# A fused four-layer kernel: the setup of the weights and the first split of rows and context, made one block

## The chip, the cores and the metric

One core of a Trainium2 chip runs the whole program. The metric is the device time of one execution in microseconds (us), the median of several runs. The engines are PE (TensorE; its weight loads are PEld), DVE (VectorE), ACT (ScalarE), POOL (GpSimd) and SP (SyncE, which here only issues DMAs). SPq and ACTq are the instruction queues of SP and ACT, seen while they issue DMAs.

## The reference

Two cross-attention layers and two feed-forward layers on 32 sequences of 128 rows with 128 channels, with a context of 32 times 77 rows:

```
x = x + tanh(g_xattn[0]) * L0_xattn(layernorm(x), ctx, ctx)        # 16 heads of 8
x = x + tanh(g_ffn[0])   * L0_ffn(layernorm(x))                    # ternary weights, depthwise conv, silu
x = x + tanh(g_xattn[1]) * L1_xattn(ctx, layernorm(x), mask)       # 16 heads of 64
x = x + tanh(g_ffn[1])   * L1_ffn(layernorm(x))                    # 8 experts, top 2
weight_quant(w): scale = 1 / clip(mean(|w|), 1e-5); clip(round(w * scale), -1, 1) / scale
```

The precision of float32 is kept by splitting each operand of a product into a high half in float16 and a low half (the rest, in float16).

## The kernel before

The program is a row of blocks. At the end of a block all engines meet at a barrier. Inside a block each engine runs its own instructions in the order in which they are written, and semaphores order them against each other. The blocks that matter here are the first four:

1. `setup` loads everything. SP issues x in four parts, `w1`, `w2`, `w3` of the experts (`nat_moe`, `nat_w3`), then the context (`ctx`), and once all has landed it clears an 18 MB table in HBM (`tokens`). ACT issues 24 small and middle-sized loads (gates, feed-forward weights, the projections of both layers) before it computes anything. DVE takes the statistics of x and their inverse root (`rstd`), then sums the absolute feed-forward weights (`absum`); PE adds that sum over partitions (`bank[7]`), and DVE quantises the weights and makes the three conv taps (`tap_w`).
2. Still in `setup`, weights are turned. There is a list `tiles`; for tile k PE transposes into PSUM bank `k % NB`, ACT copies the high half out of the bank (`hi_done`), DVE takes the low half out of the bank (`lo_done`, for tiles that have one), and PE may use the bank again for tile k + NB when both have been counted. After the tiles come four products of `q1t` and `k1t` (`product_bank`) in the same ring of banks. NB is 6.
3. `split_transposed(... "split0")` normalises x and turns it, and turns the context. For a chunk k of 4 sequences DVE normalises (`normalise`), PE transposes into one of two banks, ACT copies twice (the whole in float32, the high half in float16), and POOL subtracts (`rows_xl`, the low half). The buffers are double: `normalise(k)` waits for PE's chunk k - 2, PE's chunk k waits for ACT's k - 2, ACT's for POOL's k - 2. Then the context goes the same way without DVE, while DVE takes the statistics of the context (`context_scale`).
4. `project0` makes queries, keys and values for the first attention; `attention0` follows.

In the tables of DVE below, L326 to L393 are `setup`, L440 is `normalise`, L1122 to L1128 are `context_scale`.

Of the kernel before, what the change touches and what calls it, by code (L numbers as in the profile page):

```python
# [5 lines left out]
FP16 = mybir.dt.float16  # L6
# [3 lines left out]
ALU = mybir.AluOpType  # L10
# [4 lines left out]
C = 77  # L15
H = 16
# [92 lines left out]
def setup(nc, a, w, bank):  # L109

    with Memory(nc, "setup", w.spent) as m:
# [31 lines left out]
        block = m.block()  # L143
# [32 lines left out]
        def tile_bank(k, src):  # L176
            p, t, n = src.shape
            return bank[k % NB][0:n, 0:t * p].rearrange("q (t p) -> q t p", p=p)

        def product_bank(g):  # L180
            return bank[(NT + g) % NB][:, :].rearrange("q (t p) -> q t p", p=128)

# [23 lines left out]
        def _(act):  # L206
# [21 lines left out]
            act.dma_start(nat_o0[:, 0], a["o0"]).then_inc(l1_in, 16)  # L228
            act.wait_ge(small_in, 12 * 16)
# [20 lines left out]
        def _(pe):  # L250

            pe.wait_ge(made, 2)
# [24 lines left out]
            for g in range(G):  # L277
                pe.wait_ge(hi_done, NT + g - NB + 1)
                pe.wait_ge(lo_done, lows(NT + g - NB + 1))
# [7 lines left out]
        def _(pool):  # L287
# [25 lines left out]

            pool.wait_ge(small_in, 12 * 16)
# [5 lines left out]
        def _(dve):  # L320
# [10 lines left out]
            rsqrt(dve, link, w.rstd[:], w.mv[:, :, 1], t1[:], t2[:])  # L331

# [73 lines left out]

def split_transposed(nc, w, bank, tag, jobs, before=None, after=None):


    with Memory(nc, tag, w.spent) as m:  # L410
        for at, job in enumerate(jobs):
            n, rows = job.name, job.rows
            job.normed = m.sb(f"normed_{n}", [rows, 2, CH, D]) if job.by else None
            job.whole = m.sb(f"whole_{n}", [128, 2, CH, rows])
            job.ready, job.turned, job.high, job.split = (m.sem(f"{x}_{n}") for x in ("ready", "turned", "high", "split"))
            job.banks = [bank[2 * at + u][:, 0:CH * rows].rearrange("p (c r) -> p c r", r=rows) for u in range(2)]
        chain = m.sem("chain")
        pre, post = (work(m) if work is not None else None for work in (before, after))
        block = m.block()

        def chunks(eng, job, body):


            if job.by == "vector":
                with eng.Fori(0, NCH // 4) as i:
                    for n in range(4):
                        body(i * 4 + n, n % 2)
            else:
                for k in range(NCH):
                    body(k, k % 2)  # L430

        def normalise(eng, job, k, u):
            eng.wait_ge(job.turned, k + 1)
            for c in range(CH):
                one = slice(k * CH + c, k * CH + c + 1) if isinstance(k, int) else bass.ds(k * CH + c, 1)
                if job.by == "gpsimd":
                    how = (job.rstd[:, one], job.shift[:, one], ALU.mult, ALU.add)
                else:
                    how = (job.mean[:, one, 0:1], job.rstd[:, one], ALU.subtract, ALU.mult)
                last = eng.tensor_scalar(job.normed[:, u, c:c + 1], job.src[:, one, :], *how)  # L440
            last.then_inc(job.ready, 1)

        @block.vector
        def _(dve):
            if pre is not None:
                pre(dve, linker(dve, chain))
            for job in jobs:
                if job.by == "vector":
                    chunks(dve, job, lambda k, u: normalise(dve, job, k, u))
            if post is not None:  # L450
                post(dve, linker(dve, chain))

        @block.tensor
        def _(pe):
            for job in jobs:
                def turn(k, u):
                    if job.by:
                        pe.wait_ge(job.ready, k + 1)
                    pe.wait_ge(job.high, k + 1)
                    for c in range(CH):  # L460
                        rows = job.normed[:, u, c] if job.by else job.src[:, k * CH + c]
                        last = pe.transpose(job.banks[u][:, c, :], rows, w.ident[0:job.rows, 0:job.rows])
                    last.then_inc(job.turned, 1)

                pe.sem_inc(job.turned, 2)
                chunks(pe, job, turn)

        @block.scalar
        def _(act):
            for job in jobs:  # L470
                def copy(k, u):
                    chunk = bass.ds(k * CH, CH)
                    act.wait_ge(job.turned, k + 3)
                    act.wait_ge(job.split, k + 1)
                    for dst in (job.whole[:, u], job.hi(chunk)):
                        if job.gain is None:
                            last = act.activation(dst, job.banks[u], ACT.Copy)
                        else:
                            last = act.activation(dst, job.banks[u], ACT.Identity, bias=job.bias, scale=job.gain)
                    last.then_inc(job.high, 1)  # L480

                act.sem_inc(job.high, 2)
                chunks(act, job, copy)

        @block.gpsimd
        def _(pool):
            for job in jobs:
                def low(k, u):
                    chunk = bass.ds(k * CH, CH)
                    pool.wait_ge(job.high, k + 3)  # L490
                    pool.tensor_tensor(job.lo(chunk), job.whole[:, u], job.hi(chunk), ALU.subtract).then_inc(job.split, 1)
                    if job.by == "gpsimd" and k + 2 < NCH:
                        normalise(pool, job, k + 2, u)

                pool.sem_inc(job.split, 2)
                if job.by == "gpsimd":
                    normalise(pool, job, 0, 0)
                    normalise(pool, job, 1, 1)
                chunks(pool, job, low)
# [95 lines left out]
def attention0(nc, w, bank, qst, kst, vals):  # L595
# [1559 lines left out]
```

## Time and profile before

| | us |
|---|---|
| median of 3 runs | 1308.46 (1308.11 to 1310.41) |
| the profiled execution: its time | 1310.83 |
| its span, first to last instruction | 1308.7 |
| `setup`, up to the last DVE instruction of the block | 0 to 59.1 |
| `split0` | 59.1 to 86.8 |
| `project0` | 86.8 to 135.3 |
| DVE busy in the 27.7 us of `split0` | 25.73 |
| PE, ACT, POOL busy in the same | 14.63, 14.49, 15.23 |

The profile is of one execution. A row of a timeline gives start, length, engine, source line, operation, what it writes and reads, how many instructions were merged, and in brackets how long the engine had been idle before it and what ended that.

### The profile page before, as it was taken

To read this page: it belongs to the slowest core of one execution; us is meant where nothing else is said; L and a number is where in the kernel's file an instruction comes from. 1 tells how busy PE (TensorE), PEld (TensorE's weight loads), DVE (VectorE), ACT (ScalarE), POOL (GpSimd) and SP (SyncE) were. 2 spreads that over 40 slices of the span, in tenths; PEclk is the share of its full clock that TensorE was granted. 3 is DMA by queue.
4 is the path that set the end of the run, shared out by engine and by line. 5 is a ranking of instruction groups with operands and counts; after the bars stand their busy time and mean duration, and the time that the engine had idled before them with its cause. 6 is when DMAs were issued, how large, how long until landed. Compare 5 with 4: busy or idle time off the path is not lost.

```text
span 1308.7 us, 36650 instructions
## 1 busy us (share of the span) xinstructions
PE 1035.4 (79%) x13473; PEld 815.3 (62%) x13473; DVE 878.0 (67%) x2479; ACT 876.3 (67%) x1830; POOL 879.7 (67%) x994
## 2 busy tenths in 40 slices
PE   0569899994887459999999999999999981288860
PEld 0445677772544248888887878788787860266640
DVE  5789788885886966666675667767666741266645
ACT  0559899982664548888887878878887861166540
POOL 1170799993676737768778788788878886357661
PEclk9859555556998579999999999999999985599995
DMA  9995000000222001111211322131212211222216
GB/s 219 255 284 123 8 16 15 17 17 5 38 44 49 1 1 30 31 34 27 50 33 39 47 37 57 32 62 34 51 39 39 55 34 50 79 67 78 81 35 193
DMA packets 188834, 78.67 MB, mean 60 GB/s; under 512 B 118463, under 2 KB 184938, under 8 KB 188667
## 3 DMA queue, kind: packets, MB, share of 16 engines
q1 hardware_dynamic: 168859, 62.23, 22.1%
q0 software_dynamic: 4544, 8.67, 2.2%
q10 hardware_dynamic: 15264, 5.51, 1.7%
q8 instruction: 109, 1.79, 0.6%
q14 instruction: 58, 0.48, 0.1%
HBM read 19.54 MB, written 30.47 MB: 38 GB/s over the span
## 4 chain that ended last, share of the span: by engine, by line
PE 46%; POOL 7%; issue 4%; DVE 3%; another core or an unknown queue 2%; DMA 1%; ACT 1%; SPq 1%; POOLq 0%; ACTq 0%; DVEq 0%
PE bank L1399 11%; PE bank L1445 6%; PE bank L1893 4%; PE bank L1431 4%; PE bank L1427 4%; PE bank L1428 4%; PE bank L1429 4%; PE bank L1469 3%; PE bank L1416 3%; PE bank L1905 2%; POOL tokens L1317 2%; DVE X L1988 1%; POOL attention_pl_l L1223 1%; POOL attention_pl_c L1223 1%
## 5 line engine op out<-in xcount | busy, mean ns | idle before, releaser
L1661 DVE TENSOR_REDUCE attention_negmax<-bank 128x2 f16<-128x410 f32 x256 | 137.8, 580 | 152.6 <-PE bank L1416 152.1
L1223 POOL TENSOR_TENSOR attention_pl_l<-attention_probs_l,attention_ph_l 128x512 f16<-128x512 f32 x128 | 148.4, 1159 | 89.6 <-ACT attention_ph_l L1544 86.9
L636 POOL TENSOR_TENSOR attention_probs_l<-attention_probs,attention_probs_h 77x512 f16<-77x512 f32 x128 | 145.3, 1152 | 52.8 <-ACT attention_probs_h L718 48.6
L1223 POOL TENSOR_TENSOR attention_pl_c<-attention_probs_c,attention_ph_c 77x512 f16<-77x512 f32 x128 | 147.7, 1154 | 0.0
L2010 POOL DMA_INDIRECT outputs<-layer_kv x78 | 86.7, 1112 | 65.5 <-ACT layer_kv L1946 35.5
L1431 PEld LDWEIGHTS bank<-identh,attention_negmax 128*128 128x128 f16 (+1 forms) x1024 | 83.7, 107 | 56.3 <-issue 1.0
L1399 PE MATMUL bank<-layer_kv,ah 128*128 128x128 f16 x1024 | 108.4, 220 | 11.9 <-PEq L2123 11.8
L1445 PE MATMUL bank<-attention_vh_l,attention_ph_l 128*128 128x65 f16 x512 | 95.8, 195 | 17.9 <-POOL attention_pl_c L1223 17.9
L1399 PE MATMUL bank<-v1h,layer_kv 128*128 128x256 f16 (+1 forms) x512 | 105.8, 274 | 1.5 <-DVE attention_vl_c L1668 1.5
L1655 DVE SCALAR_TENSOR_TENSOR attention_tl<-bank,attention_th 128x512 f16<-128x512 f32 x128 | 87.8, 686 | 24.3 <-ACT attention_th L1535 24.3
L1544 ACT ACTIVATE attention_probs_l<-bank 128x512 f32<-128x512 f32 x128 | 76.2, 596 | 37.0 <-PE bank L1431 35.6
L1431 PE MATMUL bank<-identh,attention_negmax 128*128 128x128 f16 (+1 forms) x1024 | 99.3, 220 | 0.0
L1427 PE MATMUL bank<-attention_th,layer_kv 128*128 128x512 f16 (+1 forms) x256 | 97.5, 381 | 2.0 <-issue 1.7
L1429 PE MATMUL bank<-attention_tl,layer_kv 128*128 128x512 f16 (+1 forms) x256 | 97.5, 381 | 0.0
L1428 PE MATMUL bank<-attention_th,layer_kv 128*128 128x512 f16 (+1 forms) x256 | 97.5, 381 | 0.0
L1445 PE MATMUL bank<-attention_vh_c,attention_ph_c 77*128 77x65 f16 x512 | 95.9, 195 | 0.0
L1445 PE MATMUL bank<-attention_vl_l,attention_ph_l 128*128 128x65 f16 x512 | 95.8, 193 | 0.0
L1445 PE MATMUL bank<-attention_vh_c,attention_pl_c 77*128 77x65 f16 x512 | 95.7, 193 | 0.0
L1445 PE MATMUL bank<-attention_vh_l,attention_pl_l 128*128 128x65 f16 x512 | 95.6, 193 | 0.0
L1445 PE MATMUL bank<-attention_vl_c,attention_ph_c 77*128 77x65 f16 x512 | 95.5, 192 | 0.0
L1399 PE MATMUL bank<-layer_kv,al 128*128 128x128 f16 x512 | 93.9, 220 | 0.0
L1399 PEld LDWEIGHTS bank<-layer_kv,ah 128*128 128x128 f16 x1024 | 84.2, 98 | 12.7 <-issue 12.2
(370 smaller groups left out, 4089.0 us busy)
## 6 DMA issues: line engine op xcount, KB each, us to landing
tokens<-blank SPq DMA_DIRECT2D x1, 18360.0 KB, 71.0
layer_kv<-tokens SPq DMA_DIRECT2D x39, 136.0 KB
ctx<-outputs SPq DMA_DIRECT2D x8, 512.0 KB, 5.7
X<-in_x SPq DMA_DIRECT2D x4, 512.0 KB, 9.3
attention_pay<-attention_pay SPq DMA_DIRECT2D x8, 256.0 KB
out<-X ACTq DMA_DIRECT2D x8, 256.0 KB, 4.6
attention_turned_h<-attention_heads_h SPq DMA_TRANSPOSE x96, 2.2
attention_turned_l<-attention_heads_l SPq DMA_TRANSPOSE x96, 2.4
```

Of the source, the lines that this page charges most:

```text
L636: pool.tensor_tensor(probs_l[:, n % SLOTS], probs[:, n % 2], probs_h[:, n % SLOTS], ALU.subtract).then_inc(p_split, 1)
L1223: last = pool.tensor_tensor(low[:, g % 2], whole[:, g % 2], high[:, g % 2], ALU.subtract)
L1399: last = pe.matmul(dst, x, y, start=i == 0, stop=i == 2)
L1427: pe.matmul(dst, kh, th[:, g], start=True, stop=False)
L1428: pe.matmul(dst, kl, th[:, g], start=False, stop=False)
L1429: pe.matmul(dst, kh, tl[:, g], start=False, stop=False)
L1431: last = pe.matmul(dst[:, h], negmax[:, g, h:h + 1].broadcast_to([S, width]), w.identh[:], start=False, stop=h == HG - 1)
L1445: last = pe.matmul(mix[:, h], x, y, start=i == 0, stop=i == len(products) - 1)
L1544: last = act.activation(dst[:, g % 2], by_key_l, ACT.Exp)
L1655: dve.scalar_tensor_tensor(tl[:, g].rearrange("p h s -> p (h s)"), bank[0][:, :], 1.0 / AS, th[:, g].rearrange("p h s -> p (h s)"), ALU.mu ...
L1661: last = dve.tensor_reduce(negmax[:, g, 2 * i:2 * i + 2], score[i], AX.X, ALU.max, negate=True)
L2010: pool.indirect_dma_start(w.outputs, bass.IndirectOffsetOnAxis(ap=rows[:, n % RX, r, 2 * D:2 * D + 2].bitcast(UINT32), axis=0), y_rows[:, ...
```

## The change

The programs of the split (`split_programs`) are taken out of `split_transposed`, and the first use of them is called from inside the setup block. Each engine does its share of the split at a fixed place among its setup instructions: ACT after its DMA issues and ahead of the tanh of the gates, DVE after `rstd` and ahead of `absum`, PE ahead of everything else, POOL ahead of the masks. The context load moves ahead of the expert weights on SP's queue. The split keeps its four PSUM banks 0 to 3, so the weight tiles use three banks, 4, 5 and 6, instead of six; `bank[7]` holds the sum. The quantised weights and the taps move from the head of the tile list to its end. The buffers of the turned rows (`xh`, `xl`) now live through the first attention, which uses them for its probabilities in place of buffers of its own.

```diff
-def setup(nc, a, w, bank):
+def setup(nc, a, w, bank, jobs):
...
-        block = m.block()
+        split = split_programs(rows_m, w, bank, jobs, after=context_scale(w))
+        block = rows_m.block()
...
-        for t in range(3):
-            tiles.append((tap_w[:, t], TAPS, w.taph[:, t], w.tapl[:, t], WS))
-        tiles.append((nat_f[:, 1].rearrange("p (t n) -> p t n", n=128), QUANT, w.w2t[:], None, 1.0))
...
+        tiles.append((nat_f[:, 1].rearrange("p (t n) -> p t n", n=128), QUANT, w.w2t[:], None, 1.0))
+        for t in range(3):
+            tiles.append((tap_w[:, t], TAPS, w.taph[:, t], w.tapl[:, t], WS))
         NT = len(tiles)
-        NB = 6
+        RING = (4, 5, 6)
+        NB = len(RING)
...
-            return bank[k % NB][0:n, 0:t * p].rearrange("q (t p) -> q t p", p=p)
+            return bank[RING[k % NB]][0:n, 0:t * p].rearrange("q (t p) -> q t p", p=p)
...
+            sp.dma_start(w.ctx[0:C], a["ctx"].rearrange("b s d -> s b d")).then_inc(ctx_in, 16)
             for i, src in enumerate((a["w1"], a["w2"])):
...
-            sp.dma_start(w.ctx[0:C], a["ctx"].rearrange("b s d -> s b d")).then_inc(ctx_in, 16)
...
             act.dma_start(nat_o0[:, 0], a["o0"]).then_inc(l1_in, 16)
+            split.scalar(act)
             act.wait_ge(small_in, 12 * 16)
...
+            pe.wait_ge(made, 1)
+            pe.wait_ge(ctx_in, 16)
+            split.tensor(pe)
             pe.wait_ge(made, 2)
             pe.wait_ge(summed, 1)
...
+            split.gpsimd(pool)
             pool.wait_ge(small_in, 12 * 16)
...
             rsqrt(dve, link, w.rstd[:], w.mv[:, :, 1], t1[:], t2[:])
+            dve.wait_ge(ctx_in, 16)
+            split.vector(dve)
 
             dve.wait_ge(ffn_in, 64)
...
-        probs_h, probs_l = m.sb("probs_h", [C, SLOTS, HG, S], FP16), m.sb("probs_l", [C, SLOTS, HG, S], FP16)
+        probs_h, probs_l = (x[0:C].rearrange("p (n h) s -> p n h s", h=HG) for x in spare)
```

DVE, the place behind the statistics of x. Before, the inverse root of x (its last step) is followed by the sum of the feed-forward weights and their quantisation:

```order
L59 SCALAR_TENSOR_TENSOR rstd<-setup_t,rstd 128x32
L334 TENSOR_REDUCE setup_absum<-setup_nat_f 128x2
L337 TENSOR_SCALAR setup_wmean<-bank 128x2
L338 RECIPROCAL setup_winv<-setup_wmean 128x2
L340 TENSOR_SCALAR setup_nat_f<-setup_nat_f,setup_winv 128x512
```

In the changed kernel the sum stands behind the whole of the split's share, whose last step is the context's `shift_c`:

```order
L59 SCALAR_TENSOR_TENSOR rstd_c<-split_t,rstd_c 77x32
L1161 SCALAR_TENSOR_TENSOR shift_c<-split_mv,rstd_c 77x32
L349 TENSOR_REDUCE setup_absum<-setup_nat_f 128x2
L352 TENSOR_SCALAR setup_wmean<-bank 128x2
L353 RECIPROCAL setup_winv<-setup_wmean 128x2
L355 TENSOR_SCALAR setup_nat_f<-setup_nat_f,setup_winv 128x512
```

So 32 normalisations, 32 statistics of the context and their inverse root have moved ahead of everything that DVE does to a weight.

PE, the head of its program. Before, the first thing is the product for the sum (`setup_ones`), then the taps:

```order
L249 UNCONDITIONAL_BRANCH [waits barrier_Pool_Activation_PE_DVE_SP_release]
L254 MATMUL bank<-setup_absum,setup_ones 128x2 [waits setup_summed,setup_made]
L274 MATMUL bank<-ident,setup_tap_w 128x128 [waits setup_quant_done]
L274 MATMUL bank<-ident,setup_tap_w 128x128 x3
L274 MATMUL bank<-ident,setup_tap_w 128x128 [waits setup_quant_done]
```

In the changed kernel that product stands behind the last transposes of the context, and the weight tiles stand behind the product; the fourth tile (`setup_nat_k`) is the first that needs a bank of an earlier tile back:

```order
L472 MATMUL bank<-ident,ctx 128x77 [waits split0_high_ctx]
L472 MATMUL bank<-ident,ctx 128x77 x3
L266 MATMUL bank<-setup_absum,setup_ones 128x2 [waits setup_summed,setup_made]
L286 MATMUL bank<-ident,setup_nat_g 128x8 [waits setup_mask_done,setup_small_in]
L286 MATMUL bank<-ident,setup_mask_f 77x32 [waits setup_mask_done,setup_small_in]
L286 MATMUL bank<-ident,setup_nat_q 128x128 [waits setup_l1_in]
L286 MATMUL bank<-ident,setup_nat_q 128x128 x3
L286 MATMUL bank<-ident,setup_nat_k 128x128 [waits setup_lo_done,setup_hi_done,setup_l1_in]
L286 MATMUL bank<-ident,setup_nat_k 128x128 x3
```

What moved: no weight is turned before the sum is there, and from the fourth tile on a tile waits for DVE's low half of the tile three before it.

## Rows read from the trace of the kernel before

**Rows 1.** The page: busy time of each engine over the span.
```profile
PE 1035.4 (79%) x13473; PEld 815.3 (62%) x13473; DVE 878.0 (67%) x2479; ACT 876.3 (67%) x1830; POOL 879.7 (67%) x994
```

**Rows 2.** Timeline of DVE, 22 to 92 us: start, length, line, operation, idle before.
```profile
22.21 1.22 DVE L334 TENSOR_REDUCE setup_absum<-setup_nat_f 128x2 f32<-128x1024 f32 x1
...
30.24 0.17 DVE L354 TENSOR_SCALAR conv_b_half<-conv_b 128x4 f32<-128x4 f32 x1
38.32 0.15 DVE L357 TENSOR_SCALAR tg<-setup_tanhs 128x1 f32<-128x1 f32 x1 [7.91 <-ACT setup_tanhs L230]
38.39 0.64 DVE L358 TENSOR_SCALAR bias<-setup_rows,setup_tanhs 128x128 f32<-128x128 f32 x1
38.96 0.27 DVE L359 TENSOR_SCALAR gain<-setup_rows,setup_tanhs 128x128 f32<-128x128 f32 x1
...
42.64 1.88 DVE L390 SCALAR_TENSOR_TENSOR tapl<-bank,taph 128x512 f16<-128x512 f32 x3
...
46.32 1.22 DVE L385 SCALAR_TENSOR_TENSOR v1l<-setup_nat_v,v1h 128x1024 f16<-128x1024 f32 x1 [1.73 <-ACT o1h L241]
...
49.46 4.88 DVE L390 SCALAR_TENSOR_TENSOR moel<-bank,moeh 128x512 f16<-128x512 f32 x8 [0.35 <-ACT moeh L243]
...
59.89 2.32 DVE L440 TENSOR_SCALAR split_normed_x<-X,mv,rstd 128x128 f32 x8 [0.77 <-PEq L465]
62.86 11.49 DVE L440 TENSOR_SCALAR split_normed_x<-X,mv,rstd 128x128 f32 x24 [0.65 <-PE bank L462]
74.27 6.27 DVE L1122 BATCH_NORM_STATS2 split_bn<-ctx 77x6 f32<-77x128 f32 x32
...
86.57 0.19 DVE L1128 SCALAR_TENSOR_TENSOR shift_c<-split_mv,rstd_c 77x32 f32<-77x32 f32 x1
```

**Rows 3.** Timeline of ACT, 0 to 62 us, two of its issues and the first computing.
```profile
6.37 6.61 ACTq L216 DMA_DIRECT2D setup_nat_k<-in_k  x1
...
31.11 5.65 ACTq L228 DMA_DIRECT2D setup_nat_o<-in_o  x1
36.79 1.28 ACT L230 ACT_TABLE_LOAD   x1 [36.79 <-issue]
```

**Rows 4.** Timeline of ACT in the split: the two copies of one chunk.
```profile
62.34 0.60 ACT L477 ACTIVATE split_whole_x<-bank 128x512 f32<-128x512 f32 x1 [4.90 <-PE bank L462]
62.83 0.59 ACT L477 ACTIVATE rows_xh<-bank 128x512 f32 x1
```

**Rows 5.** Line L491 on POOL in the split: length min/median/max in ns.
```profile
L491 POOL TENSOR_TENSOR rows_xl<-split_whole_x,rows_xh x8: 1151/1154/1213, 63.6 to 76.8; 128x512 f32 x8
```

**Rows 6.** Timeline of PE: weight tiles, products, and the first matmul of `project0`.
```profile
44.30 1.11 PE L274 MATMUL bank<-ident,setup_nat_q 128*128 128x128 f32 x4 [7.07 <-DMA setup_nat_o<-in_o]
...
47.98 3.87 PE L274 MATMUL bank<-ident,setup_nat_moe 128*128 128x128 f32 x32
...
53.88 2.92 PE L282 MATMUL bank<-setup_k1t,setup_q1t 64*128 64x128 f32 x32
...
87.85 0.61 PE L528 MATMUL bank<-rows_xh,q0h 128*128 x1 [5.05 <-PEq L518]
```

**Rows 7.** Windows, PE alone: stretch, us, PE busy, granted clock, DMA share, GB/s.
```profile
62.00:80.00 18.00, 11.11 (x48) 0.50 1.23 284
...
92.00:93.00 1.00, 1.00 (x5) 0.61 1.23 285
```

**Rows 8.** SP: issue of the context, SP's wait for it, and landing of `w1`, `w2`.
```profile
20.07 1.73 SPq L197 DMA_DIRECT2D ctx<-in_ctx  x1
...
SPq L199 <- DMA ctx<-in_ctx: 23.0, 1, 23.0
...
L194 SPq DMA_DIRECT2D setup_nat_moe<-in_w x2: 3234/3764/4293, 7.3 to 11.0; - x2
...
DMA to landing us min/median/max: 13.0/13.3/13.7
```

**Rows 9.** Timeline of DVE in `project0`: the third low half of the queries.
```profile
94.11 0.69 DVE L575 SCALAR_TENSOR_TENSOR layer_qst<-bank,project_q_high 128x512 f32 x1 [0.67 <-ACT project_q_high L551]
```

More of the change, by code:

```diff
@@ L404, in __init__, with split_programs, chunks, normalise @@
         self.by, self.mean, self.rstd, self.shift, self.gain, self.bias = by, mean, rstd, shift, gain, bias
+def split_programs(m, w, bank, jobs, before=None, after=None):
+    for at, job in enumerate(jobs):
+        n, rows = job.name, job.rows
+        job.normed = m.sb(f"normed_{n}", [rows, 2, CH, D]) if job.by else None
+        job.whole = m.sb(f"whole_{n}", [128, 2, CH, rows])
+        job.ready, job.turned, job.high, job.split = (m.sem(f"{x}_{n}") for x in ("ready", "turned", "high", "split"))
+        job.banks = [bank[2 * at + u][:, 0:CH * rows].rearrange("p (c r) -> p c r", r=rows) for u in range(2)]
+    chain = m.sem("chain")
+    pre, post = (work(m) if work is not None else None for work in (before, after))
+    def chunks(eng, job, body):
+        if job.by == "vector":
+            with eng.Fori(0, NCH // 4) as i:
+                for n in range(4):
+                    body(i * 4 + n, n % 2)
+        else:
+            for k in range(NCH):
+                body(k, k % 2)
+    def normalise(eng, job, k, u):
+        eng.wait_ge(job.turned, k + 1)
+        for c in range(CH):
+            one = slice(k * CH + c, k * CH + c + 1) if isinstance(k, int) else bass.ds(k * CH + c, 1)
+            if job.by == "gpsimd":
+                how = (job.rstd[:, one], job.shift[:, one], ALU.mult, ALU.add)
+            else:
+                how = (job.mean[:, one, 0:1], job.rstd[:, one], ALU.subtract, ALU.mult)
+            last = eng.tensor_scalar(job.normed[:, u, c:c + 1], job.src[:, one, :], *how)
+        last.then_inc(job.ready, 1)
+    def vector(dve):
+        if pre is not None:
+            pre(dve, linker(dve, chain))
+        for job in jobs:
+            if job.by == "vector":
+                chunks(dve, job, lambda k, u: normalise(dve, job, k, u))
+        if post is not None:
+            post(dve, linker(dve, chain))
+    def tensor(pe):
+        for job in jobs:
+            def turn(k, u):
+                if job.by:
+                    pe.wait_ge(job.ready, k + 1)
+                pe.wait_ge(job.high, k + 1)
+                for c in range(CH):
+                    rows = job.normed[:, u, c] if job.by else job.src[:, k * CH + c]
+                    last = pe.transpose(job.banks[u][:, c, :], rows, w.ident[0:job.rows, 0:job.rows])
+                last.then_inc(job.turned, 1)
+            pe.sem_inc(job.turned, 2)
+            chunks(pe, job, turn)
+    def scalar(act):
+        for job in jobs:
+            def copy(k, u):
+                chunk = bass.ds(k * CH, CH)
+                act.wait_ge(job.turned, k + 3)
+                act.wait_ge(job.split, k + 1)
+                for dst in (job.whole[:, u], job.hi(chunk)):
+                    if job.gain is None:
+                        last = act.activation(dst, job.banks[u], ACT.Copy)
+                    else:
+                        last = act.activation(dst, job.banks[u], ACT.Identity, bias=job.bias, scale=job.gain)
+                last.then_inc(job.high, 1)
+            act.sem_inc(job.high, 2)
+            chunks(act, job, copy)
+    def gpsimd(pool):
+        for job in jobs:
+            def low(k, u):
+                chunk = bass.ds(k * CH, CH)
+                pool.wait_ge(job.high, k + 3)
+                pool.tensor_tensor(job.lo(chunk), job.whole[:, u], job.hi(chunk), ALU.subtract).then_inc(job.split, 1)
+                if job.by == "gpsimd" and k + 2 < NCH:
+                    normalise(pool, job, k + 2, u)
+            pool.sem_inc(job.split, 2)
+            if job.by == "gpsimd":
+                normalise(pool, job, 0, 0)
+                normalise(pool, job, 1, 1)
+            chunks(pool, job, low)
+    return Programs(gpsimd, None, tensor, scalar, vector)
@@ L417, in split_transposed @@
-        chain = m.sem("chain")
-        pre, post = (work(m) if work is not None else None for work in (before, after))
-        block = m.block()
[L421 to L441, printed above, removed]
+        split = split_programs(m, w, bank, jobs, before, after)
@@ L443, in _ @@
+        block = m.block()
         @block.vector
         def _(dve):
[L445 to L451, printed above, removed]
+            split.vector(dve)
         @block.tensor
         def _(pe):
[L455 to L466, printed above, removed]
+            split.tensor(pe)
@@ L468, in _ @@
         @block.scalar
         def _(act):
[L470 to L483, printed above, removed]
+            split.scalar(act)
@@ L485, in _ @@
         @block.gpsimd
         def _(pool):
[L487 to L499, printed above, removed]
+            split.gpsimd(pool)
```

44 lines of the change are left out of this document (19 added, 25 removed).

## The prediction

> **What bounds the kernel now.** I read the page first, for the shares [rows 1]: no engine is busy all the time, so each stage has to be read by itself. The change touches the first 87 of 1308.7 us and nothing in the body of a later stage, so I then read the timelines of this head, engine by engine, and asked which engine's chain reaches its end last. It is DVE. Up to 22 us DVE waits for x and takes its statistics. From 22.21 it sums, quantises and makes the taps, until 30.24 + 0.17 = 30.41; then it is idle for 7.91 us, because ACT gives it the tanh only at 38.3 [rows 2]. ACT is that late because it issues loads until 31.11 + 5.65 = 36.76; four of its issues take 4.4 to 6.6 us each (first and last of them in [rows 3]), and then it loads its table for 1.28 us. From 38.32 to 86.57 + 0.19 = 86.76 DVE has hardly a gap: the barrier 0.77, the first PE chunk 0.65, two waits of 1.73 and 0.35 [rows 2]. In the split DVE goes at 11.49 / 6 = 1.92 us per chunk of four sequences, while ACT needs 1.1 [rows 4], POOL 1.15 [rows 5] and PE 1.11 (four transposes at the low clock, [rows 6]). So the head is as long as DVE's work from the moment when ACT can answer it, plus waits. The question is whether the change gives DVE more to do before ACT is free, and what new waits it gets afterwards.
>
> **The change, step by step, along DVE.**
>
> Start. After `rstd` at 22.2 DVE normalises chunks 0 and 1 (2.32 us for 8 instructions without POOL beside it, [rows 2]) and, as PE turns the first two, chunks 2 and 3. It is done by 28. Chunk 4 needs PE's chunk 2, and that needs ACT's copies of chunk 0, which come behind all of ACT's issues. None of those is added or removed. So DVE now idles from about 28 to 41, and what filled 22.2 to 30.4, the quantisation, is pushed behind. Before it did 8.2 us of useful work while ACT was busy; now 4.6 us.
>
> ACT: free at 36.79, table 1.28 (the change needs the same table once more, as its load now stands in a loop body that runs twice; at chunk 4 ACT has slack of 0.8 us per chunk, so I cost it at nothing; if the slack were gone it would be 1.28). Copies of chunk 0: from 62.34 to 63.42, 1.08 [rows 4]. So 39.15. PE's chunk 2: 1.11 and 0.05 to start, 40.3. DVE's start after PE: 0.65 [rows 2]. **41.0**.
>
> Chunks 4 to 7 with POOL beside: 4 x 1.92 = 7.7, **48.6**. Statistics of the context: 74.27 to 86.76 = 12.5 [rows 2], **61.1**. ACT, PE and POOL run the context's chunks under this and end at about 58 (6.6 us of ACT behind chunk 7), so they don't count.
>
> Weights: sum, PE's product, quantisation, taps: 22.21 to 30.41 = 8.2, **69.3**. Tanh group and head copies: 38.32 to 42.64 = 4.3, less 0.37, because the 0.64 of `bias` would be the 0.27 of its neighbour `gain` when POOL is idle [rows 2]: 3.95, **73.25**. Low half of the gate weights 0.15 (the size of `tg`): **73.4**.
>
> The ring. PE could have turned weights from 58 on. It can't: its queue holds the product for the sum, which comes at 62, and then tile 3 needs bank 4 back, so DVE's low half of tile 0, at 73.4. Before, six banks and an earlier place in DVE's program let PE run ahead. From 73.4 PE turns tiles 3, 4, 5 (0.87 each: from 44.30 to 47.98 stand four groups and one single transpose [rows 6]), the single one of `nat_o0` (0.2), and the first expert tile 1.11; ACT copies it in 0.6; with 0.2 of handovers DVE begins at 73.4 + 2.6 + 0.2 + 1.1 + 0.6 + 0.2 = **78.1**. The two long low halves (2 x 1.22) lie under this wait. Nineteen tiles follow (7 `moe`, 4 `w3`, 1 `w2t`, 3 taps, 4 products). With banks to spare DVE sets the pace, 4.88 / 8 = 0.61 each. With three banks a bank must go round PE, ACT, DVE before it is free: PE 3 x 0.12 + 0.27 = 0.63 for four transposes at the high clock (3.87 / 32 = 0.12 apart), ACT 0.60, DVE 0.68, handovers 0.2: 2.1, so 0.70 per tile. The products have 8 PE rows of 0.09 each, which adds 0.1 per tile. 78.1 + 19 x 0.70 + 0.4 + 0.68 = **92.5**. I take the high clock from about 78 on: in this trace dense transposes that began at 44.30 ran 0.42 long (1.11 for four) and from 47.98 on 0.27. After 73.4 PE is about as dense (0.84 busy of 0.87).
>
> The block's end moves from 86.76 to 92.5: **+5.7**. The barrier that is gone (0.77) and the first chunk's latency (0.65) are already in, since I followed DVE directly.
>
> `project0`: before, PE starts cold; the granted clock is 0.50 from 62 to 80 and rises within 92 to 93 [rows 7], five us after the first matmul at 87.85 [rows 6]. After, PE comes out of dense tiles. DVE's only gap by this is the 0.67 before its third low half of queries [rows 9]; I take **-0.7**, between 0 (its own start hangs on other things) and -1.9 (the first round of `project0` takes 7.25 us of PE, the later ones about 5.35).
>
> SP: the context's load, 1.23 MB, moves ahead of three loads of 1 MB. `w1` and `w2` stood behind x at 7.3 and landed 13.0 and 13.7 after issue [rows 8]. The context takes their place, so about 22 to 25. DVE and PE wait for it, and up to 31 this is hidden, as ACT is not free before 37. The expert weights land later, up to the 44.8 at which all has landed now (20.07 + 1.73 + 23.0), and are needed at 76. The clearing of `tokens` starts at 45 as before. The shared buffers of the first attention change addresses and no order: nothing.
>
> Sum: +5.7 - 0.7 = **+5.0**. The profiled execution took 1310.83, 2.1 over its span, and the median of the runs is 1308.46; a shift of the head moves all three alike, so 1308.46 + 5.0 = **1313.5**.
>
> **A rule weighed.** POOL and DVE get in each other's way: with POOL at work the 24 normalisations take 0.48 each, without it the first 8 take 0.29 [rows 2]. The Trainium skill (SBUF: State Buffer, "SBUF: two separate sides") says that a DVE instruction in a two-port mode and a POOL instruction exclude each other for a whole instruction. By strict exclusion a chunk would take 4 x 0.29 + 1.15 = 2.3 us; the trace has 1.92. The sum goes by 1.92; by the rule it would be 4 x 0.4 = 1.6 us more.
>
> **The rivals.**
>
> A, the forecast: +2.7 to +7.5, the ring at the high clock for all of it (78.1 would be 77 and the end 91) or with the clock rising late. Chance 0.50.
>
> B, the ring costs nothing: handovers or PE are shorter than I think, or DVE's backlog covers them, so DVE keeps 0.61 from 75.9 on (73.4 + 2.44): 75.9 + 0.3 + 19 x 0.61 = 87.8, that is +1.0 - 0.7 = +0.3, 1308.8. For it: before, DVE kept this pace over 19 tiles. Against it: it had six banks. Chance 0.20.
>
> C, the clock stays low in the ring: 2.6 per round, 0.87 per tile, products 1.04: 78.1 + 19 x 0.87 + 0.7 + 0.7 = 96, +9.3, and nothing back in `project0`: 1317.8. For it: in the split, with PE busy 11.11 of 18 us, the clock was 0.50 throughout [rows 7]. Against it: the tiles at 44 to 48 raised it. The Trainium skill (TensorE: Matmul & The Clock Gate, "A second HAM failure mode: psum-queue depth-cycling") describes this: PE that idles briefly as it cycles through PSUM banks falls back to the low clock again and again. No row of the tiles with six banks shows it. Chance 0.12.
>
> D, faster: ACT is free earlier. [...] Each us earlier is a us off DVE's 41.0, down to 28. It decides from 5.0 + 2.6 = 7.6 us earlier on, ACT free at 29.2; at the limit of 8.8 it gives 1304.7. Against it: the same bytes are under way at the same time. Chance 0.07.
>
> E, the context lands late: it took until 44.8 before. DVE would start there: 44.8 + 2.32 + 0.65 + 11.49 = 59.3 in place of 48.6, +10.7 more: 1324. Against it: it was last in the queue then, and `w1` in its new place landed after 13.0. Chance 0.05.
>
> F: something past 140 us moves by more than 0.2% through the new buffers. Nothing speaks for it. 0.06, both signs.
>
> **Numbers.** 0.2% is 2.6 us, about what a measurement tells from no change: 1305.8 to 1311.1. Faster: D and a third of F, 0.09. Same: B, the low edge of A (0.03), a third of F: 0.25. Slower: the rest, 0.66. Range: B, A and C hold 0.82; with a little below B for port collisions that fall away (up to 0.35 x 4 = 1.4 us): 1307.4 to 1319. A's own range: 1311.2 to 1316.
>
> **What would show it.** Right: ACT's first copy at 38; DVE idle between 28 and 41; the context's last statistics at 61; no weight tile but the first three before 73; expert tiles 0.70 apart; first matmul of `project0` near 93.6. Wrong: ACT's last issue ends elsewhere than 36.8; DVE or PE is released by the context's load; low halves 0.61 or 0.87 apart; or a different length between the first matmul of `attention0` and the end.

## The result, and the profile after

| | before | after |
|---|---|---|
| median, same chip (5 runs each) | 1308.46 us | 1321.84 us (1318.36 to 1324.38) |
| ratio | | 1.0092, 95% interval 1.0078 to 1.0106 |
| profiled execution: time, span | 1310.83, 1308.7 | 1323.43, 1321.7 |
| first matmul of `project0` | 87.85 [rows 6] | 100.74 |
| from there to the end of the span | 1220.85 | 1220.96 |

The changed kernel is 13.4 us slower, and the forecast was +5.0. The last two lines of the table say where to look: all of the loss lies ahead of `project0`, 12.9 us, in the stretch that the prediction went through step by step. The page is nearly that of before [rows 1], so it is of no help here:

```profile
PE 1035.1 (78%) x13473; PEld 813.9 (62%) x13473; DVE 879.7 (67%) x2479; ACT 880.0 (67%) x1831; POOL 879.1 (67%) x994
```

The one count that differs there is ACT's, 1831 in place of 1830: the second table load.

The timeline of DVE in the head answers to [rows 2]. Columns: start, length, engine, line, operation, tiles, count, idle time before and who ended it.

```profile
24.10 2.32 DVE L452 TENSOR_SCALAR split_normed_x<-X,mv,rstd 128x128 f32 x8 [1.02 <-PEq L475]
41.14 2.29 DVE L452 TENSOR_SCALAR split_normed_x<-X,mv,rstd 128x128 f32 x8 [14.72 <-PE bank L472]
44.86 4.61 DVE L452 TENSOR_SCALAR split_normed_x<-X,mv,rstd 128x128 f32 x8 [1.43 <-PE bank L472]
49.91 2.29 DVE L452 TENSOR_SCALAR split_normed_x<-X,mv,rstd 128x128 f32 x8 [0.43 <-PE bank L472]
52.11 6.27 DVE L1155 BATCH_NORM_STATS2 split_bn<-ctx 77x6 f32<-77x128 f32 x32
...
64.48 2.11 DVE L59 SCALAR_TENSOR_TENSOR rstd_c<-split_t,rstd_c 77x32 f32<-77x32 f32 x1
...
67.41 1.21 DVE L349 TENSOR_REDUCE setup_absum<-setup_nat_f 128x2 f32<-128x1024 f32 x1
...
75.43 0.17 DVE L369 TENSOR_SCALAR conv_b_half<-conv_b 128x4 f32<-128x4 f32 x1
...
79.46 0.16 DVE L405 SCALAR_TENSOR_TENSOR wgt<-bank,wgt 128x8 f16<-128x8 f32 x1
79.54 1.22 DVE L400 SCALAR_TENSOR_TENSOR v1l<-setup_nat_v,v1h 128x1024 f16<-128x1024 f32 x1
80.67 1.22 DVE L401 SCALAR_TENSOR_TENSOR o1l<-setup_nat_o,o1h 128x1024 f16<-128x1024 f32 x1
83.39 0.29 DVE L405 SCALAR_TENSOR_TENSOR o0l<-bank,o0h 128x128 f16<-128x128 f32 x1 [1.50 <-ACT o0h L252]
84.29 0.69 DVE L405 SCALAR_TENSOR_TENSOR moel<-bank,moeh 128x512 f16<-128x512 f32 x1 [0.61 <-ACT moeh L252]
...
89.41 0.69 DVE L405 SCALAR_TENSOR_TENSOR moel<-bank,moeh 128x512 f16<-128x512 f32 x1 [0.16 <-ACT moeh L252]
...
98.93 0.69 DVE L408 SCALAR_TENSOR_TENSOR al<-bank,ah 128x512 f16<-128x512 f32 x1 [0.74 <-ACT ah L255]
```

Read it against the forecast. DVE's second row was to stand near 27 and stands at 41.14, behind 14.72 us idle. The statistics of the context start at 52.11 (forecast 48.6) and the block of weights at 67.41 (61.1), so 3.5 us were lost before them and 2.8 in them. From 67.41 to 79.46 + 0.16 it is as forecast: 8.2 and 4.0 us. The ring from there to 99.62 takes 20.0 (19.1).

ACT's timeline [rows 3], and PE's first chunk:

```profile
19.67 6.83 ACTq L225 DMA_DIRECT2D setup_nat_g<-in_wg  x1
...
37.19 2.39 ACTq L236 DMA_DIRECT2D setup_nat_o<-in_o  x1
40.97 1.28 ACT L486 ACT_TABLE_LOAD   x1 [40.97 <-PE bank L472]
...
49.72 1.28 ACT L486 ACT_TABLE_LOAD   x1 [2.71 <-PE bank L472]
```
```profile
39.77 1.94 PE L472 MATMUL bank<-ident,split_normed_x 128*128 128x128 f32 x8 [39.77 <-ACTq L491]
```

ACT is free at 37.19 + 2.39 = 39.58, not at 36.8. And PE's first transposes, whose rows lie ready since 26.4, wait for ACT: L491 is `act.sem_inc(job.high, 2)`, the count that says "both banks are free", and ACT comes to it only behind its last issue. The second table load has 2.71 us of ACT's idle time ahead of it and no wait of DVE behind it (DVE's next chunk starts at 49.91), so nothing on DVE's path to the statistics waits for it.

PE in the ring, and POOL while DVE is in the statistics:

```profile
68.82 0.56 PE L266 MATMUL bank<-setup_absum,setup_ones 128*128 128x2 f32 x2 [6.85 <-DVEq L350]
...
79.77 1.09 PE L286 MATMUL bank<-ident,setup_nat_k 128*128 128x128 f32 x4 [8.97 <-DVE wgt L405]
```
```profile
60.45 3.22 POOL L499 TENSOR_TENSOR rows_cl<-split_whole_ctx,rows_ch 128x308 f16<-128x308 f32 x4
63.61 0.24 POOL L328 CAST setup_mask_f<-setup_mask_u 32x77 f32<-32x77 uint8 x1
63.94 0.26 POOL L329 TENSOR_SCALAR setup_mask_f<-setup_mask_f 32x77 f32<-32x77 f32 x1
64.26 2.28 POOL L330 CAST mask<-setup_mask_rows 128x2464 f16<-128x2464 uint8 x1
```

The place of the ring is as forecast: PE waits 8.97 us for DVE's first low half. The second group is the loss in the statistics: DVE's L59 at 64.48 takes 2.11 us in place of the 0.19 of the same line elsewhere, and ends as POOL's cast of the masks does (66.59 and 66.54).

The same meeting of DVE and POOL shows in the normalisations. The eight that start at 44.86 take 4.61 us beside two pairs of POOL's low halves, the other groups of eight 2.29 to 2.32 with POOL idle beside them:

```profile
43.56 2.27 POOL L499 TENSOR_TENSOR rows_xl<-split_whole_x,rows_xh 128x512 f32 x2 [38.25 <-ACT rows_xh L486]
46.11 2.26 POOL L499 TENSOR_TENSOR rows_xl<-split_whole_x,rows_xh 128x512 f32 x2 [0.27 <-ACT rows_xh L486]
```

### The profile page after: what moved, and what is told of

The parts are those of the page before. It is cut to its first block, busy times and chain, and to the rows that moved or that the text cites. A ratio compares the mean times of both kernels' runs of the same rounds, so it can differ in the third digit from the quotient of the medians.

```text
span 1321.7 us, 36642 instructions
## 1 busy us (share of the span) xinstructions
PE 1035.1 (78%) x13473; PEld 813.9 (62%) x13473; DVE 879.7 (67%) x2479; ACT 880.0 (67%) x1831; POOL 879.1 (67%) x994
## 4 chain that ended last, share of the span: by engine, by line
PE 45%; POOL 7%; issue 4%; DVE 4%; DMA 1%; SPq 1%; ACT 1%; another core or an unknown queue 1%; POOLq 0%; DVEq 0%; ACTq 0%
PE bank L1426 11%; PE bank L1472 6%; PE bank L1920 4%; PE bank L1458 4%; PE bank L1454 4%; PE bank L1455 4%; PE bank L1456 4%; PE bank L1496 3%; PE bank L1443 3%; PE bank L1932 2%; POOL tokens L1344 2%; DVE X L2015 1%; POOL attention_pl_l L1250 1%; POOL attention_pl_c L1250 1%; POOL attention_rstd L1281 1%
## 5 line engine op out<-in xcount | busy, mean ns | idle before, releaser
L669 POOL TENSOR_TENSOR rows_xl<-attention_probs,rows_xh 77x512 f16<-77x512 f32 x128 | 145.1, 1152 | 53.7 <-ACT rows_xh L751 49.3
L1426 PE MATMUL bank<-layer_kv,ah 128*128 128x128 f16 x1024 | 108.9, 220 | 11.9 <-PEq L2150 11.8
L1426 PEld LDWEIGHTS bank<-layer_kv,ah 128*128 128x128 f16 x1024 | 84.6, 98 | 12.7 <-issue 12.2
```

The costliest lines, as they stand in the source:

```text
L669: pool.tensor_tensor(probs_l[:, n % SLOTS], probs[:, n % 2], probs_h[:, n % SLOTS], ALU.subtract).then_inc(p_split, 1)
L1426: last = pe.matmul(dst, x, y, start=i == 0, stop=i == 2)
```

## The experiments

All are edits of the changed kernel, unless it is said otherwise. "Head" is the start of the first matmul of `project0` in the profiled execution. ACT free is the end of ACT's last issue, x done the start of the context's statistics, "low 0" DVE's low half of the gate weights, with which the ring starts. The interval is that of the ratio to the kernel before on the same chip.

| run | ACT free | x done | low 0 | head | ratio, 95% interval |
|---|---|---|---|---|---|
| before, again | 36.22 | | | 88.18 | 1.0000 (0.9991 to 1.0009) |
| before, three banks | 35.38 | | | 91.53 | 1.0018 (1.0009 to 1.0027) |
| changed, again | 40.73 | 53.26 | 80.59 | 101.96 | 1.0086 (1.0072 to 1.0100) |
| weights first | 39.75 | 52.28 | 71.50 | 92.71 | 1.0028 (1.0016 to 1.0040) |
| six banks | 39.87 | 52.40 | 79.72 | 95.58 | 1.0041 (1.0027 to 1.0054) |
| masks first | 39.63 | 55.18 | 79.67 | 100.56 | 1.0103 (1.0087 to 1.0118) |
| count early | 39.42 | 50.83 | 78.16 | 98.95 | 1.0091 (1.0076 to 1.0107) |
| context last | 37.66 | 50.19 | 77.54 | 98.92 | 1.0069 (1.0055 to 1.0082) |
| layer 1 on SP | 30.87 | 43.40 | 70.63 | 91.92 | 1.0072 (1.0058 to 1.0086) |
| the same, again | 32.89 | 45.42 | 72.64 | 93.47 | 1.0056 (1.0038 to 1.0075) |
| weights, banks, count | 38.64 | 50.04 | 69.28 | 84.65 | 0.9980 (0.9968 to 0.9991) |
| all four | 31.22 | 44.69 | 63.79 | 79.33 | 0.9937 (0.9924 to 0.9951) |

The head of a run less that of before (88.18) should be the difference of the medians. It is, within 2.8 us, in every row but the first run of layer 1 on SP (head +3.7, median +8.8).

**The changed kernel again**, unchanged.

> The changed kernel once more, nothing edited: the yardstick for the runs beside it. The five runs so far spread from 1318.4 to 1324.4, six times the spread of the kernel before. Theory 1 (DVE's place in the program: weights and statistics pushed behind ACT's late start) says that the head ends between 95 and 100 us, and that the spread comes from the time at which ACT's last DMA issue ends (39.6 in the first profile against 36.8 before). Rival: the spread comes from later stages; then the head ends at 99.6 again while the whole time differs by up to 5 us.

Measured: 1315.15 against 1304.1, +11.05 us; DVE idle 15.34 us until 42.29. The loss is there again, somewhat smaller. The head, 101.96, lies past the expected 95 to 100, and x is done 12.53 us behind ACT free as before. The head is longer than in the first profile and the whole is 6.7 us shorter in the median, because the stretch behind the head took 1211.8 us in place of 1221.0. So the difference between the two measurements lies behind the head, as the rival had it; what makes it isn't shown.

**Weights first.** DVE's sum, quantisation and taps go back ahead of the split, and PE's product for the sum with them.
```diff
+            dve.wait_ge(ffn_in, 64)
+            link(dve.tensor_reduce(absum[:], nat_f[:], ...))
+            ...
             dve.wait_ge(ctx_in, 16)
             split.vector(dve)
-            dve.wait_ge(ffn_in, 64)
-            ...
```

> One part undone: DVE sums, quantises and makes the taps (8.2 us, 67.4 to 75.6 in the changed kernel) right behind the statistics of x, ahead of the split, and PE's product for the sum stands ahead of the split. Theory 1, DVE is the bound and was idle for 14.7 us while ACT issued loads: the 8.2 us fall into that idle time and the head ends 8.2 us earlier, at about 91.4, the whole 8 us faster than the changed kernel, ratio to the kernel before about 1.003. Rival, ACT or PE sets the end of the head: no more than 2 us.

Measured: 1306.98, the head 9.25 us shorter than in the changed kernel of the same chip; 0.98 of that is ACT, which happened to be free earlier, and 8.3 is the work. DVE's idle time until its third and fourth chunk:

```profile
31.56 2.33 DVE L451 TENSOR_SCALAR split_normed_x<-X,mv,rstd 128x128 f32 x8 [0.33 <-issue]
41.31 2.29 DVE L451 TENSOR_SCALAR split_normed_x<-X,mv,rstd 128x128 f32 x8 [7.42 <-PE bank L471]
```

So DVE's 8.2 us of work fit whole under ACT's issues and cost nothing there. Where they are put is worth 8.3 us.

**Six banks.** The ring gets the split's first three banks too, once the split is through with them.
```diff
-        RING = (4, 5, 6)
+        RING = (4, 5, 6, 0, 1, 2)
...
+            pe.wait_ge(jobs[1].high, NCH + 2)
```

> One part undone: the ring of the weight tiles has six banks again (4, 5, 6 and, as the split is over by then, 0, 1, 2; PE waits for the last copy of the context, done long before). Theory 1 with the ring as sized in the prediction: expert low halves of DVE 0.61 us apart in place of 0.73, no wait of 1.5 ahead of the first, head shorter by 5.5 us (99.6 to 94). Rival, DVE's own work sets the pace and three banks cost nothing: less than 1 us.

Measured: 1309.32; from low 0 to the last low half 14.7 us in place of 20.2. No wait is left ahead of `o0l` and fifteen low halves stand 9.72 / 15 = 0.65 us apart, from 82.27 to 91.99:

```profile
82.07 0.28 DVE L406 SCALAR_TENSOR_TENSOR o0l<-bank,o0h 128x128 f16<-128x128 f32 x1
82.27 1.27 DVE L406 SCALAR_TENSOR_TENSOR moel<-bank,moeh 128x512 f16<-128x512 f32 x2
...
85.40 2.48 DVE L406 SCALAR_TENSOR_TENSOR moel<-bank,moeh 128x512 f16<-128x512 f32 x4 [0.16 <-ACT moeh L252]
87.80 2.47 DVE L406 SCALAR_TENSOR_TENSOR w3l<-bank,w3h 128x512 f16<-128x512 f32 x4
```

**Before, with three banks.** The kernel before, its ring alone cut.
```diff
-        NB = 6
+        RING = (4, 5, 6)
+        NB = len(RING)
```

> The kernel before with only its ring of tiles cut from six banks to three (banks 4 to 6, the order of the tiles and all else as before). If the ring is a cost of its own (0.12 us a tile, and 5.5 us over the ring as the run with six banks gave back), head + 4 to + 6 us and ratio 1.003 to 1.0045. Rival: in the kernel before the ring starts long before its last tiles and VectorE is not waiting for TensorE there, so that three banks cost under 1 us.

Measured: +2.65 us in the median, +3.35 in the head, below what was expected. The pace is that of the changed kernel (50.45 to 55.57 for seven expert tiles, 0.73 each), and the wait ahead of the first expert tile is there too (0.60). But PE began its tiles early here: the wait ahead of `o0l` is 0.16 us in place of 1.50, and `w2t` and the taps stand ahead of this part of the ring, so that fewer tiles pay:

```profile
51.30 1.97 DVE L391 SCALAR_TENSOR_TENSOR moel<-bank,moeh 128x512 f16<-128x512 f32 x3 [0.16 <-ACT moeh L244]
53.43 1.97 DVE L391 SCALAR_TENSOR_TENSOR moel<-bank,moeh 128x512 f16<-128x512 f32 x3 [0.16 <-ACT moeh L244]
```

**Before, again**, as a control.

> The kernel before, unchanged, profiled beside the others: where does the +13.4 us of the first measurement, and the +11 us of the repeat, lie? In the first pair of profiles the stretch behind project0's first matmul was as long in both kernels (1220.85 and 1220.96 us), and in the later profiles of the changed kernel and its variants it was 1211.8 to 1214.4 us. If the whole difference lies in the head, the stretch behind that matmul is 1212 +- 1 us here too, and the head about 90 us long. Rival: the head is as before (87.9 us) and the rest about 1214.5 us, so that the changed kernel gives 2 us back behind the head.

Measured: head 88.18, the rest 1214.7 us. The head of before differs by 0.33 us between its two profiles. The numbers are those of the rival, but its conclusion, that the changed kernel gives 2 us back behind the head, doesn't follow. The rest is 2.9 us longer than in the changed kernel's second profile (1211.8, on another chip), but it is also 1.9 us longer than in the kernel before with three banks on the same chip (1212.9), which has the same code there; and in the first pair it was equal in both kernels. Variants of the changed kernel had 1211.8 to 1214.4, and 1219.3 on the chip on which before's median was 1309.25. So such differences come with chip and execution, as far as these profiles show, and no part of the change was tied to them.

**Masks first.** POOL casts the masks ahead of its part of the split.
```diff
+            pool.wait_ge(small_in, 12 * 16)
+            link(pool.tensor_copy(mask_f[:, 0], mask_u8[:]))
+            ...
+            pool.tensor_copy(w.mask01[:]..., mask_rows[:]).then_inc(mask_done, 1)
             split.gpsimd(pool)
```

> POOL converts the masks ahead of its share of the split, while it has nothing else to do. In the changed kernel one DVE instruction of the context's inverse root takes 2.11 us in place of 0.19 beside the 2.28 us conversion on POOL. Theory 2, DVE with two operands in SBUF and POOL exclude each other for a whole instruction: that instruction is 0.19 again, the head 1.9 to 2.3 us shorter, while the shorter stalls beside the context's subtractions (0.4 to 0.6 each) stay. Rival, the 2.11 is something else that this DVE instruction waits for: no change.

Measured: nothing gained. The masks land only at 40.54, so the cast runs at 41.19, beside the third and fourth chunk. POOL and DVE there:

```profile
41.19 2.24 POOL L329 CAST mask<-setup_mask_rows 128x2464 f16<-128x2464 uint8 x1
```
```profile
41.19 5.80 DVE L452 TENSOR_SCALAR split_normed_x<-X,mv,rstd 128x128 f32 x8 [13.99 <-PE bank L472]
```

The eight normalisations that take 2.29 us in the changed kernel take 5.80, beside the cast and two of POOL's low halves. x was done 15.55 us behind ACT free in place of 12.53, 3.0 later; the context's statistics then took 12.5 us (55.18 to 67.71) in place of 15.4, 2.9 less. The collision moved with the cast and kept its size, which shows the cause and takes away this remedy. The Trainium skill (SBUF: State Buffer, "SBUF: two separate sides") states that POOL and a DVE instruction in a two-port mode, or one with two SBUF inputs beside a POOL instruction that reads SBUF, lock each other out for a whole instruction; the rows agree, above all the 2.11 us of an instruction with two such inputs beside a cast of 2.28.

**The count early.** ACT adds `high`'s first two ahead of its issues.
```diff
         def _(act):
+            for job in jobs:
+                act.sem_inc(job.high, 2)
             act.dma_start(gates[:, 0:2] ...
...
-            act.sem_inc(job.high, 2)
```

> In the split ACT opens its two buffers for PE by a count of 2 that it adds when it reaches the split, after its DMA issues; so PE's first chunk started at 39.77 us although DVE had it ready at 26.4. Here ACT adds that count at the head of its program. Theory 1: PE turns chunks 0 and 1 at 25 to 28, DVE has chunks 2 and 3 ready by 29, and only ACT's own lateness is left; DVE's last normalisation ends 0.8 to 1.5 us earlier, and so does the head. Rival, the late opening is what the head waits for: 4 us or more.

Measured: PE starts at 25.89 and DVE does chunks 2 and 3 at once, as the prediction had it for the change itself:

```profile
24.68 2.32 DVE L456 TENSOR_SCALAR split_normed_x<-X,mv,rstd 128x128 f32 x8 [1.86 <-PEq L479]
27.30 2.30 DVE L456 TENSOR_SCALAR split_normed_x<-X,mv,rstd 128x128 f32 x8 [0.29 <-PE bank L476]
```

x is done 11.4 us behind ACT free in place of 12.53, so the count is worth 1.1 us. The median doesn't show that (1.0091 beside 1.0086), with intervals of 2 us to each side.

**The context last** on SP's queue, as before; only DVE's and PE's context parts wait for it.
```diff
-            sp.dma_start(w.ctx[0:C], ...).then_inc(ctx_in, 16)
             for i, src in enumerate((a["w1"], a["w2"])):
...
+            sp.dma_start(w.ctx[0:C], ...).then_inc(ctx_in, 16)
```

> The context's load goes back behind the expert weights on SP's queue, and DVE and PE wait for it only ahead of its statistics and of its turning. Theory 3, the order on SP's queue made ACT's issues 2.8 us longer in all: ACT's last issue ends at about 36.8 again instead of 39.6 to 40.7, and the head is 2.8 us shorter, unless the context (landed at 44.8 in the kernel before) holds up its statistics, which start at 52. Rival, ACT's issue time varies by itself or comes from something else: it ends at 39.5 or later and nothing is gained.

Measured: 1311.64. ACT's long issue, that of the 4 KB load `nat_g`, is short again (4.31 us; 6.83 in the changed kernel), and ACT is free at 33.76 + 3.90 = 37.66, between the 36.8 that was expected and the rival's 39.5:

```profile
19.50 4.31 ACTq L225 DMA_DIRECT2D setup_nat_g<-in_wg  x1
...
33.76 3.90 ACTq L236 DMA_DIRECT2D setup_nat_o<-in_o  x1
```

Not one of ACT's instructions differs from the changed kernel's. So the order on SP's queue has a part in how long ACT's issues take. The context's own landing held up nothing: its statistics start 12.53 us behind ACT free, as in the changed kernel. No unchanged copy of the changed kernel ran on this chip; by the ratios (1.0069 beside 1.0086 and 1.0092, with intervals that overlap) the order is worth 2 to 3 us.

**Layer 1's five transfers on SP** in place of ACT, behind the expert weights.
```diff
-            act.dma_start(nat_q1[:], a["q1"]).then_inc(l1_in, 16)
-            ...
+            sp.dma_start(nat_q1[:], a["q1"]).then_inc(l1_in, 16)
+            ...
```

> SP instead of ACT issues the five loads of the second attention's weights, behind the expert weights, so ACT reaches the split when its small loads are issued, at about 32.5 us. Theory 1, the split is held up by ACT's issues alone: all of the head moves by the same, 6 to 7 us, and the kernel is 6 to 7 us faster than the changed one (ratio to the kernel before about 1.003). Rival, the loads' landing or PE's and DVE's own work is the bound: less than 2 us.

> The changed kernel with the five transfers of layer 1 issued by SP, a second time. The profile of its first run had a head 10 us shorter than the changed kernel's, but that run was the fastest of its five and the medians were only 2 to 4 us apart. If ScalarE's issues are worth what the profile showed, the head is 92 +- 1 us again and the median falls to 1.002 (an earlier head by 10 us, behind it 1212 us). If the profiled run was a lucky one, the head is 95 to 98 us and the ratio 1.006 to 1.007 again.

Measured: ACT free at 30.87 and 32.89, x done 12.53 us behind it both times, heads 91.92 and 93.47, which is 8.5 to 10 us shorter than in the changed kernel's second profile (101.96). The medians followed by less: ratios 1.0072 and 1.0056 beside 1.0086 to 1.0092, some 2 to 5 us. The second run fits its own head (+5.3 us, median +6.7); the first doesn't, and its profiled execution was its fastest by 3 us. The expected 1.002 was not reached, and what holds the median of the first run up is not shown.

**Weights, banks and count; and all four** with layer 1 on SP.

> Weights first, six banks and the preset count early, but ScalarE issues all its transfers as in the changed kernel. If the issues on ScalarE's queue set when the split starts, the context's statistics start at 50 to 51 us instead of 44.7, and the head is 5 to 7 us longer than that of the run with all four edits (79.3): about 85 us, ratio 0.998 to 1.000. Rival, from the run in which the issues alone were moved (the head 10 us shorter in the profile, the median only 4 us): the median loses 2 to 3 us only, ratio 0.996.

> Weights first on DVE, six banks, ACT's count at its head, and the five loads on SP, all together. By theory 1 DVE is never idle for long from 23 us on, and the head ends at 99.6 - 8 - 6 - (4 to 6) = 80 to 82, against 86.8 in the kernel before: 4 to 6 us faster than before, ratio 0.995 to 0.997. Rival, the parts overlap and share one gain (DVE's idle time of 14.7 us is all that there is to win, plus the ring): head at 84 or later, ratio 0.998 or more.

Measured: 1301.42 and 1294.35, ratios 0.9980 and 0.9937. All four together are 8.1 us faster than before in the median, more than was expected, with the head at 79.33 in place of 88.18. The fourth edit is worth 5.3 us of head and 0.43% here, as expected; its rival, 2 to 3 us, didn't hold. With it ACT is free at 31.22, just as DVE is through with the weights and begins x at 31.11, and DVE's wait of 14.72 has gone:

```profile
33.72 2.31 DVE L456 TENSOR_SCALAR split_normed_x<-X,mv,rstd 128x128 f32 x8 [0.28 <-PE bank L476]
37.44 4.62 DVE L456 TENSOR_SCALAR split_normed_x<-X,mv,rstd 128x128 f32 x8 [1.41 <-PE bank L476]
```

## Why the prediction was wrong

The direction and the mechanism were right: DVE does less before ACT is free, and the ring of three is slower. The size was 8.4 us short. Two terms failed most, by 2.8 us each: the time at which ACT is free, and the statistics of the context. By the steps of the prediction, for the first pair:

| step | forecast | measured | missing |
|---|---|---|---|
| ACT free | 36.8 | 39.58 | 2.8 |
| from there until x is done | 11.8 | 12.5 | 0.7 |
| statistics of the context | 12.5 | 15.3 | 2.8 |
| weights, tanh group, copies, low 0 | 12.3 | 12.2 | -0.1 |
| ring, to the last low half | 19.1 | 20.0 | 0.9 |
| `project0`, to the first maximum of `attention0` | -0.7 | +0.3 | 1.0 |

These make 8.1 of the 8.4 us.

**ACT free: the first failed step.** "None of those is added or removed" is true of ACT's issues and does not fix their length. The prediction counted issues and took their durations over unchanged, while it moved 1.23 MB on the queue next door; its rival D priced an ACT that is free earlier, and nothing priced one that is free later. Measured: 35.4 to 36.8 in the three profiles with before's order, 38.6 to 40.7 in the seven with the changed order and all issues on ACT, 37.66 with the context put back. That last run, together with the long issue that is short in all four profiles with the context last, shows the order to be a cause. How much of the 2.8 it makes is less sure, as single profiles of one order differ by 1.4 to 2.1 us. The forecast of the loads failed in another place too: all had landed by 37.90 in place of 45.05, where the prediction had them land at 44.8, and the clearing of `tokens` began then. No run ties time to this. What follows ACT follows it exactly: x was done 12.53 us behind ACT free in seven profiles, from 30.87 to 40.73.

**"It is done by 28": the second.** PE's first two chunks wait for ACT's count, which stands at the start of ACT's part of the split, so behind its issues. The prediction had looked at who fills the banks, not at who first calls them free. It cost 1.1 us: chunks 2 and 3 land in the time in which DVE should have gone on with chunk 4. From there to x done the four chunks took 52.11 - 44.86 = 7.25 us in place of 7.7: beside POOL a pair took 4.61, which is the 2.3 a chunk of the prediction's strict exclusion, and not 1.92 each; but the other pair had POOL idle and took 2.29. The two errors offset each other, so only 0.7 is missing in the sum, in part by luck.

**The statistics at 12.5: the third.** The duration was taken from a place where POOL's work ended at 84.50, and only two instructions of DVE's reciprocal root lay beside it:

```profile
83.04 0.77 DVE L54 TENSOR_SCALAR split_t<-split_t 77x32 int32<-77x32 int32 x1
83.84 0.69 DVE L55 TENSOR_SCALAR rstd_c<-split_t 77x32 int32<-77x32 int32 x1
```
```profile
83.01 1.49 POOL L491 TENSOR_TENSOR rows_cl<-split_whole_ctx,rows_ch 128x308 f16<-128x308 f32 x2 [0.19 <-ACT rows_ch L477]
```

In the new block POOL's context halves end at 63.67, not at about 58, and the masks' cast stands right behind them. The prediction took 0.37 us off `bias` because the cast wouldn't lie beside it any more [rows 2], and didn't ask where the cast would lie. Both come on top of the root: 2.11 for 0.19 once, and 0.58 to 0.74 for 0.19 in four others. Of the 2.8 us, 1.9 are the cast's and 0.9 come from the halves. The run with masks first shows the cast's part; the part of the halves is read from the timeline alone.

**The ring** was right in place and nearly in size: first expert tile 4.7 us behind the end of low 0, as forecast, 5.12 / 7 = 0.73 apart (0.70); the rest is in the tile without a low half and in the products, with waits of 0.84 and twice 0.74. Rival B, a ring for nothing, is refuted by the six banks' 5.5 us and by the 3.35 us in the kernel before. Rival C, the low clock for all of the ring, is refuted by the lengths: four transposes take 0.63 us from 85.13 on.

```profile
85.13 0.63 PE L286 MATMUL bank<-ident,setup_nat_moe 128*128 128x128 f32 x4 [0.20 <-ACT moeh L252]
```

The granted clock couldn't have refuted it. PE in the new ring, columns stretch, us, busy, granted clock, DMA share, GB/s:

```profile
80.00:84.00 4.00, 4.00 (x20) 1.00 1.22 284
84.00:89.00 5.00, 4.30 (x30) 1.00 1.24 287
89.00:100.00 11.00, 7.94 (x64) 1.00 1.22 282
```

It reads 1.00 from the start, and yet the groups of four at 79.77, 80.64 and 81.50 took 1.09, 1.06 and 1.06 us. In the kernel before it is the same: it reads 1.00 in every stretch from 44 to 49 us, and the groups of four up to 47.8 took 1.11 and 1.06. So the prediction's "the tiles at 44 to 48 raised it" isn't what the rows say; the transposes got faster there at an unchanged reading, and why is not shown.

**`project0`'s -0.7** did not come. PE starts at a granted clock of 0.97 (100.7 to 101.5 us), but then it reads 0.50 from 101.5 to 104, and 1.00 again from 105 on. DVE's first low half starts 3.35 us behind the first matmul both before (91.19 - 87.85) and after:

```profile
100.74 0.39 PE L561 MATMUL bank<-rows_xh,q0h 128*128 x1 [2.47 <-PEq L551]
```
```profile
104.09 0.87 DVE L608 SCALAR_TENSOR_TENSOR layer_qst<-bank,project_q_high 128x512 f32 x1
```

The matmul took 0.39 in place of 0.61 [rows 6], and DVE's start didn't hang on it: its second memset stands 2.20 us behind its first before (91.06 and 88.86) and 2.21 after (103.96 and 101.75), and the low half 0.13 behind that. What spaces the two memsets was not tried. The wait of 0.67 that was forecast to go did go, so that the third low half of the queries stands 2.17 us behind the first in place of 2.92 [rows 9]; by the fifth the gain was gone (5.93 and 5.98).

**Right:** DVE's work of 8.2 us pushed behind ACT's issues was the largest cost, and the weights-first run gives 8.3 back. Rival E, a late context, did not happen: its statistics started behind DVE's own work.

## What to carry to other kernels

Before moving work, ask what it was hiding under: here 8 us of weight work were free only because another engine was busy issuing transfers, and the three edits that restore cover, banks and count turn a loss of 13 us into a small gain. An engine's time spent in issuing transfers was no constant of its own program here: it moved with what SP's queue held. When programs of two blocks are put into one, walk each semaphore's first increment (who says "free", and behind what does that stand?), and lay the moved work beside POOL's timeline, not only its own engine's.

## What the runs showed of the hardware

The issue of one load of 4 KB on ACT's queue (`nat_g`) took 4.3 to 5.0 us with the context last on SP's queue (four profiles) and 6.8 to 7.5 with it behind x (ten profiles), ACT's issues up to there being the same. A cast of 2.24 us on POOL, moved beside the normalisations, put off x by 3.0 us, more than its own length, as the normalisations that it held up then lay beside two low halves. And the granted clock read 1.00 from 62 to 100 us while four transposes took 1.09 us at 79.77 and 0.63 at 85.13: in these traces the pace of PE is told by the lengths of its rows, and the reading alone doesn't tell it.
